# Moving the slots of a pipelined selective-scan kernel: gate and transposes back, statistics and products to other steps

## The reference, cut to what matters

```python
# layer 0, for each of 2 sequences of 2048 tokens, D = 512, DI = 1024, N = 16 states
xn = layernorm(x) * (1 + scale) + shift
x_in, z = split(xn @ in_proj_w.T)              # 1024 channels each
u  = silu(causal_conv4(x_in) + conv_b)
dt_r, B, C = split(u @ x_proj_w.T)             # 64, 16, 16
dt = softplus(dt_r @ dt_proj_w.T + dt_proj_b)
h_t = h_{t-1} * exp(dt_t * A) + (dt_t * u_t) * B_t      # 16 states per channel
y_t = sum_n h_t[n] * C_t[n] + u_t * D_param
x1 = x + gate * ((y * silu(z)) @ out_proj_w.T)
# layer 1, on x1: an efficient attention (softmax of q over features, of k over time), layernorm, silu, product
```

## Time and profile before

| | us |
|---|---|
| median of 3 runs (lowest, highest) | 2515.31 (2513.39, 2518.91) |
| the profiled execution | 2515.61 |
| its span, first to last instruction | 2513.8 |
| first step to last step of the loop | 69.4 to 2014.7 |
| DVE busy | 2097.6 (83%) |
| PE busy | 2096.4 (83%) |
| POOL busy | 1891.8 (75%) |
| ACT busy | 1707.2 (68%) |
| mean granted TensorE clock | 0.91 |

### The profile page before, as it was taken

One profiled execution on the slowest core, in us unless ns is written; L12 is line 12 of the kernel. 1 busy time (PEld: TensorE's weight loads), 2 busy tenths in 40 slices (PEclk: granted clock), 3 DMA queues, 4 the chain that ended last, 5 costly groups with the idle time before them and its releaser, 6 DMA issues. The chain is left out here.

```text
span 2513.8 us, 29512 instructions
## 1 busy us (share of the span) xinstructions
PE 2096.4 (83%) x9536; PEld 1383.4 (55%) x9536; DVE 2097.6 (83%) x2299; ACT 1707.2 (68%) x3332; POOL 1891.8 (75%) x1175
## 2 busy tenths in 40 slices
PE   9877788778877887887778877886887889999999
PEld 3344455445444544554445444544544479988887
DVE  3988988899889998888888898889899966676666
ACT  3678676877687777777776787778655545556655
POOL 0698898889889989998998899989999832222325
PEclk9898789888998998899889898989897899999999
DMA  6510231032004110412041004110410211112113
GB/s 229 215 38 26 85 105 38 25 118 81 30 26 148 51 34 26 152 46 68 22 152 51 28 23 152 43 30 22 164 42 1 82 64 32 32 45 68 47 51 118
DMA packets 78072, 176.46 MB, mean 70 GB/s; under 512 B 7453, under 2 KB 10781, under 8 KB 77918
## 3 DMA queue, kind: packets, MB, share of 16 engines
q1 hardware_dynamic: 77918, 174.56, 20.9%
HBM read 157.23 MB, written 17.30 MB: 69 GB/s over the span
## 5 line engine op out<-in xcount | busy, mean ns | idle before, releaser
L1450 POOL TENSOR_TENSOR arena<-arena 128x1024 f32<-128x1024 f32 x512 | 1200.8, 2360 | 198.5 <-ACT arena L603 174.2
L1038 DVE TENSOR_TENSOR_SCAN arena<-ps,arena 128x512 f32<-128x512 f32 x1024 | 1233.2, 1251 | 15.4 <-POOL arena L1415 7.9
L603 ACT ACTIVATE ps<-arena 128x512 f32<-128x512 f32 x1087 | 719.5, 681 | 424.7 <-DVE arena L1038 352.6
L322 PE MATMUL ps<-keep,arena 128*128 128x128 f32 x4096 | 597.0, 297 | 299.8 <-POOL arena L1450 292.7
L322 PEld LDWEIGHTS ps<-keep,arena 128*128 128x128 f32 x4096 | 512.8, 153 | 483.5 <-POOL arena L1450 390.3
L272 PE MATMUL ps<-arena 128*128 128x512 f32 x1024 | 512.8, 649 | 44.8 <-issue 43.6
L1023 DVE TENSOR_TENSOR arena<-ps,arena 128x1024 f32<-128x1024 f32 x448 | 538.5, 1202 | 2.8 <-DMA arena<-scr_bc 1.5
L272 PEld LDWEIGHTS ps<-arena 128*128 128x128 f32 x1024 | 205.2, 211 | 277.3 <-issue 276.1
L603 ACT ACTIVATE arena<-arena 128x2 f32<-128x2 f32 (+2 forms) x599 | 229.0, 385 | 35.1 <-DMA arena<-in_x 10.9
L1397 POOL TENSOR_TENSOR arena<-arena 128x512 f32<-128x512 f32 x168 | 214.0, 1274 | 39.2 <-ACT arena L603 32.2
L312 PE MATMUL ps<-arena 128*128 128x512 f32 x512 | 235.3, 600 | 0.0
(11 more groups left out here) (148 smaller groups left out, 2811.2 us busy)
## 6 DMA issues: line engine op xcount, KB each, us to landing
arena<-scr_bc SPq DMA_DIRECT2D x128, 512.0 KB, 6.0
arena<-in_inT SPq DMA_DIRECT2D x128, 256.0 KB, 2.7
arena<-in_x SPq DMA_DIRECT2D x17, 512.0 KB, 4.1
scr_x<-arena SPq DMA_DIRECT2D x32, 256.0 KB, 2.0
arena_b<-scr_x SPq DMA_DIRECT2D x16, 512.0 KB, 3.7
arena_c<-scr_x SPq DMA_DIRECT2D x32, 256.0 KB, 2.9
out<-arena_c SPq DMA_DIRECT2D x32, 256.0 KB, 2.1
arena<-in_x SPq DMA_DIRECT2D x30, 256.0 KB, 3.6
```

Of the source, the lines that this page charges most:

```text
L322: last = e.matmul(YP[:, 128 * q:128 * q + 128], hb[G % R][:, i, 128 * q:128 * q + 128], ident, start=(g == 0 and i == 0 and q == 0), stop= ...
L603: return e.activation(o_, i_, f, **kw)
L1038: e.tensor_tensor_scan(H, DA[s % 4], H, h0, MUL, ADD).then_inc(v_sc)
L1450: e.tensor_tensor(H, H, Ct[:, GN * g:GN * g + GN, :], MUL).then_inc(g_w)
```

## The change

It changes the tables, one order and one condition. The tail of the y pipeline moves: the copy from step 5 to 6, the back transposes from 7 to 9, the gate from 8 to 13. In `softplus` the rectified step size (Relu, which frees the bank) is issued right behind the absolute value, ahead of the exponential. The z products, their activation (now at step 0 of the next unit, two units at a time as before), the output products and tiles, the statistics and the transposes of the next x get other steps; the two products that prepare the second layer's scales move from unit 7 to unit 2. Nothing is computed otherwise, and no operation is added or removed.

```diff
-        AT = {..., "yt": 5, "yb": 7, "yf": 8, ...}
+        AT = {..., "yt": 6, "yb": 9, "yf": 13, ...}
-        ZMM = {(1, 8): 1, (1, 10): 2, (3, 8): 1, (3, 11): 2, (5, 6): 1, (5, 10): 2, (7, 10): 1, (7, 13): 2}
-        ZSILU = {(1, 15): (1, 2), (3, 14): (1, 2), (5, 14): (1, 2), (7, 14): (1, 2)}
-        STATS = {(0, 1): 0, (1, 0): 1}
-        RS1 = {(0, 2): 0, (0, 13): 1}
-        SQ = {(0, 7): 0, (1, 3): 1}
-        RS = {(0, 5): 0, (1, 6): 1}
-        NORM = {(0, 9): 0, (1, 12): 1}
-        NTR = {(0, 10): 0, (2, 1): 1}
-        NEV = {(0, 15): 0, (2, 2): 1}
-        OUTM = {(0, 8): 0, (0, 10): 4, (1, 1): 8, (1, 4): 12, (2, 2): 16, (2, 7): 20, (2, 10): 24, (2, 12): 28}
-        OUTA = {(0, 14): 0, (1, 9): 1, (2, 11): 2, (3, 1): 3}
+        ZMM = {(1, 11): 1, (1, 14): 2, (3, 10): 1, (3, 13): 2, (5, 9): 1, (5, 13): 2, (7, 11): 1, (7, 14): 2}
+        ZSILU = {(2, 0): (0, 1), (4, 0): (0, 1), (6, 0): (0, 1), (0, 0): (0, 1)}
+        STATS = {(0, 1): 0, (1, 4): 1}
+        RS1 = {(0, 2): 0, (1, 4): 1}
+        SQ = {(0, 7): 0, (1, 8): 1}
+        RS = {(0, 8): 0, (1, 8): 1}
+        NORM = {(0, 12): 0, (1, 13): 1}
+        NTR = {(0, 15): 0, (2, 0): 1}
+        NEV = {(1, 0): 0, (2, 1): 1}
+        OUTM = {(0, 7): 0, (0, 13): 4, (1, 3): 8, (1, 5): 12, (2, 2): 16, (2, 5): 20, (2, 9): 24, (2, 11): 28}
+        OUTA = {(1, 2): 0, (1, 9): 1, (2, 8): 2, (2, 15): 3}
-        CC = [(7, 4), (7, 9)]
+        CC = [(2, 7), (2, 12)]
...
                 act(spt, BG[bank_of["dt", U]], ACT.Abs).then_inc(a_abs)
-                e.wait_ge(a_abs, U + 1)
-                act(spt, spt, ACT.Exp, scale=-1.0).then_inc(a_ex)
-                e.wait_ge(a_ex, U + 1)
-
                 if U == 2:
                     e.wait_ge(v_0, 3)
                 elif U > 2:
                     e.wait_ge(g_du, U - 2)
                 if U:
                     act(dt[U % 2], BG[bank_of["dt", U]], ACT.Relu).then_inc(a_rl)
+                e.wait_ge(a_abs, U + 1)
+                act(spt, spt, ACT.Exp, scale=-1.0).then_inc(a_ex)
+                e.wait_ge(a_ex, U + 1)
                 act(spt, spt, ACT.Ln, bias=1.0).then_inc(a_ln)
...
-                if (j, pr) in ZSILU:
+                if U > 0 and (j, pr) in ZSILU:
```

More of the change, by code:

```diff
@@ L151, in program @@
         after = lambda k, n: ((16 * k[0] + k[1] + n) // 16, (k[1] + n) % 16)
-        AT = {"dt": 4, "soft": 7, "add": 6, "du": 7, "copy": 12, "yt": 5, "yb": 7, "yf": 8, "proj": (6, 14), "xdbl": (7, 3)}
+        AT = {"dt": 4, "soft": 7, "add": 6, "du": 7, "copy": 12, "yt": 6, "yb": 9, "yf": 13, "proj": (6, 14), "xdbl": (7, 3)}
         XMM = {(3, 0): 0, (3, 4): 1, (4, 2): 2, (4, 8): 3, (4, 13): 4, (5, 0): 5, (5, 14): 6, (6, 7): 7}
```

## The result

| | before | after |
|---|---|---|
| median of 4 runs (lowest, highest), us | 2514.43 (2513.39, 2518.91) | 2417.33 (2414.27, 2419.34) |
| ratio, 95% interval | | 0.9609 (0.9593 to 0.9626) |
| the profiled execution, its span | 2515.61, 2513.8 | 2414.27, 2412.5 |

The change makes the kernel 97 us faster. The time lies inside the range of the prediction (2342 to 2450), 47 us above its point and in the interval of the rival "the coupling eats half".

The account below looks back on a forecast made before the run. It took DVE's stop at the gate, starving DVE and POOL, as the bound: 2515.6 - 181.0 (gate) + 11.4 (POOL) + 21 (coupling) + 3.2 (loop end) = 2370.2 us, range 2342 to 2450.

Parts of the forecast that it names:

- the coupling eats half: Rival: normalization and output products in units 0 to 2 cost 11.6 us a chunk, 81 in place of 21; 2430; chance 0.28.
- What bounds the kernel, and the gate (-181): DVE's gate waits for PE's back transposes, 181.0 us in 55 waits; five steps later, all of it goes.
- What is late next: POOL: A chunk can't be shorter than the busier of DVE and POOL; POOL's excess in chunks two to seven returns, +11.4 us.
- The coupling (3 us a chunk, +21): Moved normalization, output products and z activations together cost 3 us a chunk in seven chunks, +21 us; upper ends 22.8 a chunk.
- The moved normalization (0 to 4.4): First unit of a chunk: ACT would wait about 4.4 us for POOL's later arithmetic, costing 0 to 4.4 us a chunk.
- The z activations (near 0): At step 0 on ACT, ahead of keeping the last group, delaying POOL's product: 0 to 14.8 us a chunk, near 0.
- Relu first (nothing): Relu ahead of the exponential in softplus frees its bank 0.6 us earlier: 0 to 0.1 us in 64 units, taken as nothing.
- The end of the loop (+3.2): Last unit: PE stands until the later gate frees its bank, so layer 1 starts 3.2 us later; between 0 and 5.
- PE waits for L1058: Sign that the forecast would be wrong: PE waiting for DVE's gate (L1058) in the profile after.
- The rule weighed: If the shared SBUF port blocked POOL during DVE's scans and expands: at most 17 us in seven chunks, 2387; 1 in 20.
- The change doesn't do what it says: Rival: POOL's lag grows until the transposes are as late as before relative to step 13; about 2515; chance 0.05 ("unchanged").
- The banks: Rival: back transposes hold a BG bank until step 13, PE stands 34 us a chunk; slower, 2590; chance 0.05.

Follow-up runs that it names:

- The edit to POOL's adds: Kernel after with POOL's add of the convolution's oldest tap cut to 1 of 512 columns in units 3 to 6, result not the reference's: 2370.96 us.
- five single edits to after: Kernel after with one expand a unit on POOL (2414.82), x product later (2416.05), keeping before z (2419.37), squares earlier, normalization later (2417.68), or old softplus order (2414.03).
- the old slots with the late gate: Kernel before with only the y tail moved (copy at step 6, back transposes 9, gate 13): 2421.44 us, ratio 0.9617.

## Why the prediction was right or wrong

**What bounds the kernel, and the gate (-181): right.** The gate's waits fell to 1.2 us, and its slots alone give the gain within what can be told. The working had 5.2 us to spare at step 13 in unit 17, and step 10 does as well in time. But the term says only that DVE no longer stops there. That PE, ACT and POOL would be in time for a DVE that never stops was the matter of the next terms.

**"What is late next: POOL" (+11.4): the step that failed.** It took a chunk's length as the larger total of two engines, and that from windows of 232 to 253 us. Those are equal within 0.3 us in three of the chunks two to seven and gave +11.4 in all, where the idle time of DVE in the third chunk alone is 12.0 us. Totals can't show that POOL falls behind in units 3 and 4, when DVE never stops: its lag reaches 13.3 us in unit 5, where DVE then waits for ACT and for PE's sums to free one of the six buffers. A comparison by unit points that way but wouldn't have given the size. From the trace before it adds up to 223.8 us, 4.0 above POOL's total. The edit to POOL's adds speaks for this reading (8.6 us less for POOL, a chunk 6.6 us shorter); dropping its expands at j = 7 doesn't (4.6 us less for POOL, 2.0 more for DVE, and nothing gained in that chunk). So where POOL's work lies counts, and by which rule it makes the chunk's length isn't shown.

**The coupling (3 us a chunk, +21): the term that was mis-sized.** DVE's idle time outside the gate was 16.8 us in the loop and is 90.9: 74 us more, against the 32.4 of the two terms together. The difference of 42 is nearly all of the 44 us by which the profiled execution (2414.3) missed the sum (2370.2). The prediction asked only what the moved pieces add, in units 0 to 2 (and the z activations), and there the 21 us that it took were not far off: DVE's idle time outside the gate in those units, in all eight chunks, went from 5.1 to 38.2 us, and L1037 waits 13.8 us for ACT in them (5.1, 0 and 8.7), where it named about 20. It had no term for unit 5: 30.8 us of waits for ACT and PE, where 35.9 us of waits at the gate had been. Unit 7 adds another 7.7 (11.7 outside the gate before, 19.4 now). The stop at the gate had been POOL's chance to catch up in that unit, and the chain ACT, POOL, PE that kept DVE waiting had been hidden behind it. The reason for staying near 0, that "DVE's scans lose only 15.4 us in 64 units", was read from a kernel in which DVE stopped in 55 of them. Such a row says nothing of a DVE that doesn't. The coupling was a known rival with 0.28; that the time still lies in the range is owed to the range's width, which took most of that rival in.

**The moved normalization (0 to 4.4): right in size, wrong in worth.** ACT waits 3.6 us there in the third chunk, predicted 4.4, but taking it away changes nothing that can be told (2417.68).

**The z activations (near 0): not refuted.** POOL's products wait 8.3 us for ACT in the third chunk, 18.7 before; predicted under 8. Putting the keeping ahead of them gave no time.

**Relu first (nothing): right**, by the runs with the old order.

**The end of the loop (+3.2): right.** The last part takes 502.4 us from the last scan, 499.1 before; with the old steps in the last unit it takes 499.3. The first product of layer 1 comes 8.8 us behind the last scan, as named (about 9), though the prediction's own sum (2021.9 against 2014.7) gives 7.2. "PE waits for L1058" was listed as a sign against the forecast; it does, 7.7 us, in this unit, as its own working said.

**The rule weighed.** POOL's products have a median of 2360 ns, at most 2417, before 2359 and 2396, with DVE at work in 95% of the loop. The Trainium skill, "SBUF — State Buffer", section "SBUF: two separate sides", says that GpSimd and, among others, DVE work with two SBUF inputs take a shared port pair in turns, and that the one that comes second is fully blocked. These rows show no such blocking of POOL by scans and expands that read one operand from PSUM, and the 17 us that the prediction bounded it by are not there.

**The rivals.** The time is in the interval of "the coupling eats half" (2400 to 2455, 0.28), for which the prediction took 11.6 us a chunk in units 0 to 2, 81 in all. In size that is near the 74 measured; of the place less than half is right (33 us of the 74 are in units 0 to 2). "The change doesn't do what it says" is ruled out by the gate's 1.2 us. "The banks" exists as a wait, 43.3 us of PE's behind the gate in the run with the transposes at 7 and 41.9 with them at 9. It costs some 10 us at most, and not the 34 us a chunk of the rival; in after nearly nothing of it is left (1.6 us ahead of the same products), with the small products at their new steps.

**Open.** Why five single edits to after all end at 232 us in the third chunk isn't explained beyond that reading of the traces (waits taken away in one place come back in another); the old slots with the late gate have 229.1 there, and more in the first, second and last. Why dropping POOL's expands at j = 7 gives its time in the fifth chunk and not in the third isn't explained either.

## What to carry to other kernels

Where two in-order engines share the work, don't take the larger of their totals over a loop or a chunk for its length. Look where one falls behind the other, and whether the buffers between them let it catch up; here they ended at a lag of 13.3 us, in units of 28. A stop that one engine makes is slack for all the others. Before you book its removal as a gain (181 us of waits gave 97 here), add up what each of them has to do in the time that will be left, in every place where the stop was, also where the edit moves nothing. And a late step at the end of a pipelined loop has a price at its last turn (some 3 us here), which can be had back by other slots for that turn alone.
